# Router and sort moved in between the convolution's products, second mask stage moved ahead of the router, first group's first units begun a turn later

## The reference

```
x = x + conv(group_norm(x))        # info = relu(16 x 64), mask = sigmoid(16 x 64), all 256 products
                                   # mask*info, out = relu(64 x 256)
t = tokens(x);  t = t + attention(layernorm(t))   # linear attention, 8 heads, elu+1, message through
                                   # Wm, layernorm, W1 (128 x 128), relu, W2, layernorm, residual
t = t + moe(layernorm(t))          # 8 experts 64 -> 128 (gelu) -> 64; softmax router, the two best
                                   # experts of each token, each weighed by its probability
```

## Time and profile before

| | us |
|---|---|
| median of 3 runs (lowest, highest) | 1300.73 (1295.26, 1302.85) |
| profiled execution | 1301.52 |
| its span, first to last instruction | 1299.7 |
| PE busy | 1002.7 (77%) |
| DVE busy | 756.4 (58%) |
| ACT busy | 545.4 (42%) |
| POOL busy | 480.2 (37%) |
| POOL idle ahead of the scatters, until IDX is there | 331.1, in 7 waits |
| PE idle ahead of T, until the slots are loaded | 67.3, in 3 waits |

### The profile page before, as it was taken

The page is one execution under the profiler, slowest core; times in us unless marked ns, Lnnn a source line. Parts: engine busy times, 40 slices in busy tenths (PEclk is TensorE's granted clock), DMA queues, the critical chain, the costliest instruction groups (busy, mean ns, idle before and its releaser), DMA issues.

```text
span 1299.7 us, 34961 instructions
## 1 busy us (share of the span) xinstructions
PE 1002.7 (77%) x14091; PEld 628.9 (48%) x14091; DVE 756.4 (58%) x1737; ACT 545.4 (42%) x836; POOL 480.2 (37%) x482
## 2 busy tenths in 40 slices
PE   5888582877998699868897699869986899742796
PEld 2453251454655366544755466546654565531322
DVE  5554762277646765477637766586647664630255
ACT  2245230652555245542565254543555255510343
POOL 0010037002755075703763075605571385300450
PEclk7788866895999789987999699987999699965798
DMA  4530000663576446654557356653656255689311
GB/s 142 154 93 1 1 7 28 172 178 97 133 188 157 132 127 180 161 139 113 148 151 185 101 154 173 157 158 104 182 148 179 71 160 149 172 202 233 82 36 49
DMA packets 258933, 168.88 MB, mean 130 GB/s; under 512 B 156500, under 2 KB 244052, under 8 KB 258772
## 3 DMA queue, kind: packets, MB, share of 16 engines
q1 hardware_dynamic: 244436, 151.70, 43.4%
q0 software_dynamic: 14336, 14.94, 4.8%
HBM read 133.12 MB, written 33.42 MB: 128 GB/s over the span
## 4 chain that ended last, share of the span: by engine, by line
PE 44%; DVE 23%; issue 6%; SPq 5%; ACT 4%; DMA 1%; POOL 1%; DVEq 0%; ACTq 0%
PE HP L1073 4%; PE R L788 3%; PE HP L1053 3%; PE R L813 3%; PE HP L1091 3%; PE R L777 2%; DVE CWB L1752 2%; PE R L953 2%; PE R L962 2%; PE R L955 2%; PE R L842 2%; PE R L866 2%; PE R L875 2%; PE HP L1029 2%; PE HP L1040 2%
## 5 line engine op out<-in xcount | busy, mean ns | idle before, releaser
L1334 POOL DMA_INDIRECT slots_hbm<-CWB,IDX x224 | 219.8, 981 | 397.3 <-DVE IDX L1738 331.1
L1345 POOL DMA_INDIRECT CWB<-y_hbm,IDX x224 | 219.8, 981 | 223.5 <-issue 116.0
L1263 ACT ACTIVATE H<-HP 128x1024 f32<-128x1024 f32 x84 | 83.1, 989 | 204.6 <-PE HP L1053 203.2
L1752 DVE TENSOR_TENSOR CWB<-HP,CWB 128x512 f32<-128x512 f32 x84 | 55.9, 665 | 162.3 <-PE HP L1073 161.8
L1040 PE MATMUL HP<-W,CWB 128*128 128x128 f32 x322 | 59.4, 311 | 107.4 <-DMA CWB<-slots_hbm 67.3
L1053 PE MATMUL HP<-CWB 64*64 64x64 f32 x5152 | 103.7, 234 | 9.6 <-DVE OF_BLOCK L1733 5.1
L1053 PEld LDWEIGHTS HP<-CWB 64*64 64x64 f32 x5152 | 91.8, 146 | 35.9 <-issue 31.0
L1040 PEld LDWEIGHTS HP<-W,CWB 128*128 128x128 f32 x322 | 37.7, 154 | 141.2 <-issue 72.1
L1255 ACT ACTIVATE CWB<-HP 128x512 f32<-128x512 f32 x84 | 49.2, 586 | 126.9 <-PE HP L1040 126.7
L1073 PE MATMUL HP<-CWB,H 128*64 128x64 f32 x2576 | 101.5, 239 | 0.0
L1073 PEld LDWEIGHTS HP<-CWB,H 128*64 128x64 f32 x2576 | 94.4, 155 | 0.0
(11 more groups left out here) (262 smaller groups left out, 1980.6 us busy)
## 6 DMA issues: line engine op xcount, KB each, us to landing
CWB<-pairs_hbm SPq DMA_DIRECT2D x644, 128.0 KB
CWB<-slots_hbm SPq DMA_DIRECT2D x77, 132.0 KB, 2.8
CWB<-slots_hbm SPq DMA_DIRECT2D x77, 128.0 KB, 2.4
y_hbm<-CWB SPq DMA_DIRECT2D x77, 128.0 KB
X<-x SPq DMA_DIRECT2D x14, 512.0 KB, 4.4
out<-XB SPq DMA_DIRECT2D x11, 512.0 KB, 4.1
BIG<-gates_hbm SPq DMA_DIRECT2D x16, 256.0 KB, 8.3
slots_hbm<-CWB,IDX POOLq DMA_INDIRECT x224
```

The costliest lines, as they stand in the source:

```text
L1263: f(H[:, n % 2, :, some], L1.rearrange("p (r t) -> p r t", r=2)[:, :, some], ACT.Gelu).then_inc(gelu_done, 1)
L1334: nc.gpsimd.indirect_dma_start(out=slots_hbm[a % 2], in_=XFT[:, t, :], in_offset=None, out_offset=bass.IndirectOffsetOnAxis(ap=IDX[:, a % ...
L1345: nc.gpsimd.indirect_dma_start(out=YG[:, t, :], out_offset=None, in_=y_hbm[a % 2], in_offset=bass.IndirectOffsetOnAxis(ap=IDX[:, a % 2, t: ...
L1752: v.tensor_tensor(YT[:, there, :, :], YPS[:, there, :, :], SLT[:, n % 3, there, P:P + 2].unsqueeze(3).broadcast_to([P, columns(u), 2, C]), ...
```

## The change

`SCHEDULE` is re-ordered from its start to `kv_values.0`; from `numerator.0` on it is as before. Behind `group_norm` both mask stages now stand ahead of `choose_1`. `choose_2` is cut in two (`choose_2`, `choose_3`), and the router's and the sort's stages stand between the `info`, `low` and `high` stages, with `sort_3` behind `conv_out.1`, where it stood behind `low_0.0`. The letters shift too: B9 stood at `norm_1.1` and now stands at `features_1.1`, for instance. `gate_rows` is left out for all groups but the last. Turn 1 issues no T, A, B; the thirteen of group 0 (`LATE`) are issued in a row at the start of turn 2. Waits on `cwt_done` of earlier groups become waits on `lg_shifted`.

```diff
 SCHEDULE = [
-    ("channel_stats", "KA"), ("gates", "K"), ("gate_tokens", "TB"), ("gate_exp", ""), ("group_stats", "K"),
-    ("group_norm", "AK"), ("choose_1", ""), ("info_mask_0", "TB"), ("choose_2", "A"), ("classes", ""),
-    ("info_mask_1", "FT"), ("gate_rows", "B"), ("shares", ""), ("sort_1", ""), ("info_0.1", ""), ("info_0.0", "F"),
-    ("sort_2", ""), ("low_0.1", ""), ("low_0.0", "F"), ("sort_3", ""), ("high_0.1", ""), ("high_0.0", "AF"),
-    ("info_1.1", ""), ("info_1.0", "T"), ("low_1.1", ""), ("low_1.0", "B"), ("high_1.1", ""), ("high_1.0", "A"),
-    ("conv_out.1", "T"), ("conv_out.0", ""), ("centre_1.1", ""), ("store", ""), ("centre_1.0", "B"),
-    ("rstd_1", "A"), ("norm_1.0", "T"), ("norm_1.1", "B"), ("features_1.0", ""), ("features_1.1", "A"),
-    ("query.1", ""), ("query.0", "T"), ("key.1", "B"), ("key.0", ""), ("key_value.1", ""), ("key_value.0", "A"),
-    ("kv_turn.1", ""), ("kv_turn.0", ""), ("kv_values.1", ""), ("kv_values.0", "B"), ("denominator", ""),
+    ("channel_stats", "KA"), ("gates", "K"), ("gate_tokens", "T"), ("group_stats", "BK"), ("gate_exp", ""),
+    ("group_norm", "AK"), ("info_mask_0", "T"), ("info_mask_1", "B"), ("choose_1", ""),
+    ("info_0.1", "A"), ("info_0.0", "F"),
+    ("low_0.1", ""), ("low_0.0", "T"), ("choose_2", ""), ("high_0.1", "B"), ("high_0.0", "F"), ("classes", ""),
+    ("info_1.1", ""), ("info_1.0", "A"), ("sort_1", ""), ("low_1.1", "F"), ("low_1.0", "T"), ("choose_3", ""), ("gate_rows", ""),
+    ("sort_2", ""), ("high_1.1", "F"), ("high_1.0", "B"), ("shares", ""), ("conv_out.1", ""), ("sort_3", ""),
+    ("conv_out.0", ""), ("centre_1.1", "A"), ("store", ""), ("centre_1.0", "T"),
+    ("rstd_1", "B"), ("norm_1.0", "A"), ("norm_1.1", "T"), ("features_1.0", ""), ("features_1.1", "B"),
+    ("query.1", ""), ("query.0", "A"), ("key.1", "T"), ("key.0", ""), ("key_value.1", ""), ("key_value.0", "B"),
+    ("kv_turn.1", ""), ("kv_turn.0", "A"), ("kv_values.1", ""), ("kv_values.0", "B"), ("denominator", ""),
...
+LATE = [step for _, steps in SCHEDULE[LEFT:] for step in steps]
...
             done = dict(BEGUN, K=0, F=0)
+            if b == 1:
+                done = {step: 0 for step in done}
+                for step in LATE:
+                    if steps.get(step):
+                        steps[step](done[step])
+                    done[step] += 1
...
-                    if steps.get(step):
+                    if steps.get(step) and not (a == 1 and step in "TAB"):
...
-                    sp.wait_ge(cwt_done, a + 1)
+                    sp.wait_ge(cwt_done, 1)
...
-            last_read = {"L1": (cwt_done, 1), "XP": (cwt_done, 1)}
+            last_read = {"L1": (lg_shifted, G), "XP": (lg_shifted, G)}
...
                             if exists(a - 1) and a != EARLY:
-                                pe.wait_ge(cwt_done, a)
+                                pe.wait_ge(lg_shifted, nth(a, G - 1))
...
                     router_link(v.tensor_tensor(gt(2), gt(2), gt(4), ALU.add))
+
+                def choose_3():
                     dve.wait_ge(gate_exp, a + 1)
...
-                    "choose_1": choose_1, "choose_2": choose_2, "gate_rows": gate_rows,
+                    "choose_1": choose_1, "choose_2": choose_2, "choose_3": choose_3,
+                    **({"gate_rows": gate_rows} if a == DENSE else {}),
```

More of the change, by code:

```diff
@@ L116 @@
 AHEAD = [name.partition(" ")[2] for name in OPENING if name.startswith("next ")]
-ROUTER = ("gates", "gate_tokens", "gate_exp", "choose_1", "choose_2", "gate_rows")
+ROUTER = ("gates", "gate_tokens", "gate_exp", "choose_1", "choose_2", "choose_3", "gate_rows")
 SORT = ("classes", "shares", "sort_1", "sort_2", "sort_3")
@@ L992, in gate_rows @@
                 def gate_rows():
-                    pe.wait_ge(cw_done, a + 1)
+                    pe.wait_ge(cw_done, DENSE + 1)
                     if exists(a + 1) and a > 0:
@@ L1099, in dense_second @@
                     if u < len(YR):
-                        pe.wait_ge(cwt_done, a + 1)
+                        pe.wait_ge(cwt_done, 1)
                     else:
@@ L1140, in parts @@
                     **slotwise("hidden_0", lambda slots: hidden(0, slots)), **slotwise("hidden_1", lambda slots: hidden(1, slots)),
-                    **slotwise("hidden_out", hidden_out), **slotwise("centre_4", centre_4), "gates": gates, "gate_tokens": gate_tokens, "gate_rows": gate_rows,
+                    **slotwise("hidden_out", hidden_out), **slotwise("centre_4", centre_4), "gates": gates, "gate_tokens": gate_tokens,
+                    **({"gate_rows": gate_rows} if a == DENSE else {}),
                     **({"sort_1": sort_1, "sort_2": sort_2, "sort_3": sort_3} if a < DENSE else {}),
@@ L1740, in gate_rows @@
                 def gate_rows():
-                    dve.wait_ge(cwt_ps, a + 1)
+                    dve.wait_ge(cwt_ps, 1)
                     for s in range(G):
```

## The result

| | before | after |
|---|---|---|
| median us (lowest to highest) | 1298.84 (1295.26 to 1302.85, 4 runs) | 1383.08 (1381.33 to 1386.1, 4 runs) |
| profiled execution's span | 1299.7 | 1379.5 |
| mean granted clock | 0.867 | 0.851 |

The ratio is 1.065 (95% interval 1.0611 to 1.069): the change makes the kernel slower by 84 us, 19 more than the 1364 forecast. The lines quoted here are those of the kernel named; in the kernel after they stand 8 to 11 lines further down than before. Offsets are from K0, as in the prediction.

A forecast was written before the change was run, and what follows sets the result against it. No engine is full (PE 77%, DVE 58%), so the order of work bounds. Turns 2 to 6 +71.5, turn 7 +4.9, units' move −10, turn 8 −3: +63 on a 1299.7 span, giving 1364 us; range 1315 to 1400.

The forecast's parts named there:

- The front: K0 to conv_out.0 and the sort: IDX at 54.0, 12.0 later; conv_out.0 ends at 54.6, 6.4 earlier.
- The scatter, the adds, X, `after(9)`, the slots: POOL, then SP, turns 2 to 6: scatter ends 95.6, second X load 100.3, slots 106.2, T0 109.2, 12.8 later.
- the third rival: SP's queue: its order costs nothing, T0 at 99.8 in all six turns; +16, 1317 us; 12%.
- Where PE waits: Turns 2 to 6: PE idles 12 to 20 us ahead of T0, ended by the slots' load.
- T0 to K0: Turn's second half: stays 45.4 us, plus an estimated 1.5 (0 to 5) for PE's lower clock.
- Turn 2 "taken as the others": Turn 2, whose IDX comes earlier in both kernels: counted at the same +14.3 as turns 3 to 6.
- PE's arrival at T0 without the chain: conv_out.0 to T0: 35.4 us kept, T9 and A8 added (0.66 + 1.16), so PE reaches T0 at 91.9.
- The first rival: T0: the scatter doesn't bind, PE finds its slots at 91.9; −4.5 in six turns, 1261 us; 5%.
- the packed front: Front: DVE hardly idles, IDX at 46.5, T0 at 101.7; about 1310 us; 10%.
- The units' move: Turn 1 and start of turn 2: 27.59 us wait goes, LATE block takes 19.6; −10 (−14 to −4).
- Turn 7 and turn 8: Turn 7, no next_input: T0 at 99.8, +4.9 with the clock. Turn 8: T10 waits instead of T9, −3.
- The clock rival: Front: falls to the low clock, PE's work makes IDX 60; 6 more in six turns, 1400 us; 15%.

The follow-up runs named there:

- e4: Kernel after with 16 of the 32 scatters per group, so its output isn't the reference's: 1288.43 us, one run.
- e2: Kernel after with next_input called at the numerator stages instead of features_1: 1332.17 us, ratio 1.0293.
- e1: Kernel after with B9 moved back to norm_1.1, ahead of next_input: 1341.53 us, ratio 1.0345.
- e5: Kernel after without the LATE block, the first group's units begun in turn 1 again: 1387.72 us, ratio 1.072.
- f1: Kernel after with the old stage order and next_input at the numerator stages: 1290.85 us, ratio 0.9959.
- g1: f1 with POOL's residual adds waiting, from group 2 on, for DVE's reciprocal: 1283.68 us, ratio 0.9893.
- g3: Kernel before with next_input at the numerator stages and POOL's adds waiting for DVE's reciprocal from group 2: 1295.13 us, ratio 0.9987.
- g2: f2 with POOL's residual adds waiting, from group 2 on, for DVE's reciprocal: 1296.05 us, ratio 0.9986.
- f2: f1 re-ordered: second mask ahead of the router's choices, classes before low_0.0, whole sort before info_1: 1305.31 us, ratio 1.0081.
- e3: Kernel before with only B9 moved behind next_input, from norm_1.1 to features_1.1: 1330.96 us, ratio 1.0271.

## Why the prediction was right, and where its sizes were off

The direction, the chain and most offsets held. By its steps:

- **The front.** IDX forecast at 54.0, measured 55.1 (53.9 to 55.4); conv_out.0's end 54.6, measured 55.9. Right to 1.3 us. The walk through DVE's queue with durations of the earlier trace rows was good.
- **The scatter, the adds, X, `after(9)`, the slots.** Forecast 95.6, 100.3, then slots at 106.2; measured 96.4, 101.1 and 106.7. Right. e4 and e2 show that both links bind, and their worth: the third rival (SP's order free, T0 at 99.8) is e2, with T0 at 99.7 to 100.9. Its trace has 25.5 us more than the kernel before and its ratio 38, against the +16 of that rival, whose -13 for the other turns was too much (below).
- **Where PE waits: wrong by one link.** "PE idles 12 to 20 us ahead of T0, ended by the slots' load" didn't happen. I had the y store in the same group of issues, and took only its time on SP, not who waits for it. Combine 11 does, on DVE, with the reciprocal behind it. It is released 4.3 us after y store 9 is issued (534.26 to 538.54), and from there the numerator's products need 6.0 to T0: 111.8, where the slots alone would have let T0 begin at 109.7. So the wait costs 2.1 us more than the one I named. e1, which sends y store 9 early, moves the wait to T0, as it should.
- **T0 to K0.** Forecast 45.4 + 1.5, measured 46.07. PE does begin on the lower clock (T0 1.11 instead of 0.66), but has it back soon: the windows view below has a granted clock of 0.97 from T0 to K0. Together: a turn forecast at 156.1, measured 158.0 on average, +9.7 over five turns.
- **Turn 2 "taken as the others"**: before, it was 136.8, since its IDX came at 37.5. After, all turns wait for the same chain, and it is 159.2. The base of the five turns was 707.1, not 709.4: +2.3.
- **PE's arrival at T0 without the chain: 91.9 forecast, 94.2 in turn 3 of e4, mean of turns 2 to 6 95.9.** This step failed, and only the scatter hid it. From conv_out.0 to T0 I kept 35.4 and added the two products that come in (1.8); turn 3 of e4 has 38.5, its turns 2 to 6 39.3 in the mean, with waits of PE in the norm's and key's chains that I had not priced. The kernel after shows it too where PE gets to T0 unhindered: in turn 7 it arrives at 95.8 (100.6 less the wait of 4.78, not "near 8"). The first rival (1261) rested on this step, and so did the -4 that the packed front (1310) had for turn 7.
- **The units' move.** Forecast -10, measured -4.4 (turn 1). The mechanism was right, twice mis-sized: the tail without units takes 47.8 us, not 44 (202.64 to 250.40; the row below has it with the 2.06 us of the product ahead), and the block 23.1, not 19.6. With no units between, PE is sparse in that tail and part of it runs on the lower clock. The block begins on that clock (T0 1.12), and A3 waits 3.48 us. The profile names no releaser for that; SP issued unit 3's eight pair loads from 260.60 to 265.94, so the wait for these weights is the likely cause.
- **Turn 7 and turn 8.** +4.9 forecast, +5.4 measured; -3 forecast, -4.7 measured. T0 of turn 7 is at 100.6, T10 waits in turn 8.
- **The clock at the front.** The gap of 6.54 us ahead of T7 is gone. The granted clock of the front is 0.82, hardly above the 0.78 of the kernel before (414 to 475), and e4's turn 3 has 0.76 with conv_out.0's end at nearly the same offset (55.7 against 55.9): the clock didn't set the front's length. The clock rival (1400) didn't come.

Windows of the kernel after: front of turn 3, stall of turn 3, T0 to K0, tail of turn 1, LATE block; columns as in the earlier trace rows.
```profile
432.70:488.70 56.00, 46.88 (x624) 27.48 (x625) 44.09 (x110) 21.11 (x31) 0.39 (x1) 0.82 0.50 134
524.00:545.00 21.00, 6.72 (x37) 3.31 (x35) 4.04 (x6) 2.17 (x4) 8.55 (x7) 0.65 0.55 151
544.60:590.60 46.00, 38.49 (x693) 24.02 (x692) 21.78 (x53) 24.89 (x41) 29.95 (x31) 0.97 0.67 174
200.60:250.40 49.80, 33.48 (x272) 16.72 (x272) 17.52 (x43) 19.01 (x34) 19.50 (x21) 0.83 0.34 94
250.40:273.50 23.10, 17.63 (x440) 15.25 (x436) 5.83 (x10) 8.14 (x10) 0.00 (x0) 0.72 0.44 113
```
In the tail of turn 1 the clock returns in the middle of a stage, as two rows of one line show (timeline of PE, kernel after); the same stretch of the kernel before, with units in it, had 0.96 (the row of before that follows), and e5, which differs from the kernel after only in having them there, 0.97.
```profile
214.74 2.08 PE L961 MATMUL R<-XN,W1X 64*128 64x512 f32 x4 [1.34 <-DVE T L1564]
...
222.39 1.02 PE L961 MATMUL R<-XN,W1X 64*128 64x512 f32 x4
```
Windows of the kernel before, tail of turn 1:
```profile
230.80:277.20 46.40, 38.95 (x693) 24.24 (x693) 20.51 (x50) 26.18 (x42) 0.00 (x0) 0.96 0.67 178
```
The block's rows (timeline of PE, kernel after) show both its slow begin and the wait at A3:
```profile
250.43 1.12 PE L1048 MATMUL HP<-W,CWB 128*128 128x128 f32 x4
...
268.15 1.99 PE L1061 MATMUL HP<-CWB 64*64 64x64 f32 x64 [3.48 <-issue]
270.07 1.11 PE L1048 MATMUL HP<-W,CWB 128*128 128x128 f32 x4
```

The sum of the terms: forecast +63; +9.7 and +2.3 in turns 2 to 6, +5.6 for the units' move, +0.5 and -1.7 in turns 7 and 8, and +0.4: 79.8.

The page "DMA: Bandwidth & Descriptors" of the Trainium skill (section "Anatomy of one DMA") was cited for the issuing sequencer holding the wait. The trace after agrees: y store 9, whose data had been ready since DVE ended combine 9 at 505.27, went out at 534.26, right behind the X loads.

What stays open: why f1 to g1 gains what g3 doesn't, why g2 is slower than g1, and what bounds PE's arrival at T0. Four orders of the front (before, e4, f1, f2), with IDX anywhere from 40 to 56 and conv_out.0 from 55 to 61, all have it at 94 to 98 in turns 3, 5 and 6.

## What to carry to other kernels

When a step is moved past a blocked entry of an in-order queue, list everything the step issues there, and for each the buffer it frees: the store that releases a double buffer can bind before the load one is watching. Price a chain that has slack by its end, not by its start: 13 us later at IDX (41.8 to 55.1) used up 8.6 us of slack and put two links of SP's queue behind it. And don't count a stage that ends earlier as a gain before the stages after it have been walked as well: here conv_out.0 came 3 us earlier and T0 didn't.

## What the runs showed of the hardware

DVE operations are held up by POOL's adds. Timeline of DVE in turn 3 of the kernel before, with POOL's add from 497.62 to 502.29:
```profile
499.34 0.29 DVE L1589 COPY T<-R 128x129 f32<-128x129 f32 x1 [0.38 <-PE R L884]
499.55 2.79 DVE L1593 TENSOR_SCALAR KS<-W,R 128x16 f32<-128x16 f32 x1
502.25 0.28 DVE L1589 COPY T<-R 128x129 f32<-128x129 f32 x1
```
The copy out of PSUM, begun under the add, lasts its 0.29 us; the small operation that reads W in SBUF lasts 2.79 instead of 0.24, to the end of the add. It does so in six turns of the kernel before (2.57 to 3.91), and the combines of e3 and f2 (4.43, 4.68 instead of 0.42) are the same. Not every DVE operation is held. Timeline of DVE in turn 3 of g1, whose adds run from 504.90 to 509.56:
```profile
505.97 2.48 DVE L1629 TENSOR_TENSOR T<-R,T 128x512 f32<-128x512 f32 x4 [1.22 <-PE R L944]
```
These four have one input in PSUM (R) and one in SBUF (T), and last the 2.48 us that they do elsewhere. So in the kernel after, e4 and g1 no DVE operation of turns 2 to 7 is more than 1.2 us over its usual time: those that fall under the adds there all read PSUM. How long a hold lasts isn't settled: in e3 it went through both of the two adds, in turn 1 of the kernel before two operations of 0.42 us (166.37 and 168.88) were held for 2.48 and 2.46, one by each add.

The page "SBUF — State Buffer" of the Trainium skill (section "SBUF: two separate sides") describes this: DVE and GpSimd share a port pair that is an exclusive lock for a whole instruction. It names DVE operations with two SBUF inputs, against a GpSimd operation that reads SBUF as the adds do; the combine is one. Its other case is a DVE operation in a 2-port mode, and by the same page (section "Who interferes with whom") tensor_scalar can enter one. The row at 499.55 is a TENSOR_SCALAR with one SBUF tensor and a per-partition scalar, and is held, which agrees; whether it ran in such a mode the trace doesn't show.
